# Two rounded 32-bit weight pieces and one set of 32-bit codes for the built units of pass 3

## What is computed

```
def _rgcn_conv(x, src, dst, edge_type, edge_weight, W, root, bias):
    xj = x[src]
    m = 0
    for r in range(4):
        mask = (edge_type == r)[:, None]
        m = m + mask * (xj @ W[r])
    m = m * edge_weight[:, None]
    out = segment_sum(m, dst, num_segments=6250)
    return out + x @ root + bias
...
ew = (edge_weight - edge_weight.min()) / (edge_weight.max() - edge_weight.min() + 1e-08)
h = relu(_rgcn_conv(x, src, dst, edge_type, ew, W1, root1, b1))
h = _rgcn_conv(h, src, dst, edge_type, ew, W2, root2, b2)
```

## Time and profile before

| | before |
|---|---|
| median of 3 runs (lowest, highest) | 3859.27 us (3858.65, 3859.64) |
| the profiled execution, its time | 3852.48 us |
| its span, first to last instruction | 3850.6 us |
| PE busy (matmul) | 3549.2 us, 92% |
| DVE busy | 2277.3 us, 59% |
| ACT busy | 2070.9 us, 54% |
| POOL busy | 2644.1 us, 69% |
| pass 0, first to last gather | 47.1 to 1116.4 us |
| pass 3, first to last gather | 1991.0 to 2928.5 us |
| pass 4, first to last gather | 2948.2 to 3836.4 us |

### The profile page before, as it was taken

How to read it: one execution, slowest core, us unless ns; L and a number is a source line. 1 busy time by engine, 2 the same in 40 slices (tenths; PEclk the granted TensorE clock), 3 DMA queues, 4 the chain that set the end, 5 groups by cost and what they waited for, 6 DMA issues and landing times. The chain is left out here.

```text
span 3850.6 us, 70135 instructions
## 1 busy us (share of the span) xinstructions
PE 3549.2 (92%) x23444; PEld 3114.6 (81%) x23444; DVE 2277.3 (59%) x7846; ACT 2070.9 (54%) x4844; POOL 2644.1 (69%) x2744
## 2 busy tenths in 40 slices
PE   7999999999999999799978998898986999989997
PEld 5999888888887999688856777777775888888887
DVE  6999998998876555666654445554442233333332
ACT  4555555555546555566665555555545445544543
POOL 5777777777753666355547777777776777777776
PEclk8999999999999999799989999999997889999898
DMA  7666666666675666466634454445443445555453
GB/s 232 190 190 191 185 191 190 185 188 191 184 206 133 162 161 161 116 161 167 160 103 158 162 169 168 168 166 170 168 163 125 154 155 170 161 159 170 150 170 119
DMA packets 438782, 642.44 MB, mean 167 GB/s; under 512 B 266434, under 2 KB 310978, under 8 KB 438275
## 3 DMA queue, kind: packets, MB, share of 16 engines
q1 hardware_dynamic: 310322, 375.66, 30.5%
q0 software_dynamic: 100880, 235.32, 22.7%
q10 hardware_dynamic: 27202, 26.78, 2.2%
HBM read 468.80 MB, written 168.73 MB: 166 GB/s over the span
## 5 line engine op out<-in xcount | busy, mean ns | idle before, releaser
L641 POOL DMA_INDIRECT work<-table_rel,reli x1462 | 1382.6, 946 | 493.9 <-issue 438.0
L641 POOL DMA_INDIRECT work<-table_pre,srci x831 | 817.3, 984 | 263.2 <-issue 261.0
L2582 ACT ACTIVATE work<-iota,local 128x72 f32<-128x72 f32 x1464 | 377.9, 342 | 322.8 <-PE bank L1589 313.7
L1589 PEld LDWEIGHTS bank<-work 128*128 128x128 f32 x2928 | 385.8, 210 | 190.9 <-DMA work<-table_rel,reli 185.4
L1589 PE MATMUL bank<-work 128*128 128x72 f32 x2928 | 398.7, 295 | 148.6 <-DMA work<-table_rel,reli 148.2
L2587 ACT ACTIVATE work<-work,ew,src_both 128x72 f32<-128x72 f32 x1464 | 514.9, 434 | 6.1
L1357 PE MATMUL bank<-counts,piece_hi 128*128 128x432 f32 x1300 | 482.9, 371 | 35.5 <-DVE counts L1307 23.5
L1019 ACT ACTIVATE X<-bank 128x468 uint8<-128x468 f32 (+1 forms) x624 | 326.6, 543 | 266.6 <-PE bank L961 259.8
L1357 PE MATMUL bank<-counts,piece_lo 128*128 128x432 f32 x1300 | 468.9, 361 | 0.0
L922 PE MATMUL bank<-w_both,work 128*128 128x256 f32 x1664 | 433.7, 386 | 17.5 <-DVE work L856 9.2
L934 PE MATMUL bank<-work 128*128 128x64 f32 x3328 | 399.6, 274 | 7.0 <-DVE hist L803 6.2
(11 more groups left out here) (322 smaller groups left out, 6129.6 us busy)
## 6 DMA issues: line engine op xcount, KB each, us to landing
work<-ea_cols SPq DMA_DIRECT2D x208, 256.0 KB, 2.9
kept<-work SPq DMA_DIRECT2D x50, 880.0 KB
kept<-w_both SPq DMA_DIRECT2D x50, 880.0 KB
work<-kept SPq DMA_DIRECT2D x50, 880.0 KB
w_both<-kept SPq DMA_DIRECT2D x50, 880.0 KB
adj<-X SPq DMA_DIRECT2D x156, 225.0 KB
work<-adj SPq DMA_DIRECT2D x65, 540.0 KB
work<-table_rel,reli POOLq DMA_INDIRECT x1462
```

The lines of the kernel that those rows point to most:

```text
L641: pool.indirect_dma_start(into[:, u, :], None, tables[p], bass.IndirectOffsetOnAxis(ap=idx_of(p)[:, t:t + 1].bitcast(U32), axis=0)).then_i ...
L1589: mm = pe.matmul(bank[4 + m % LATE_BANKS][:, 0:PAIR_WIN], late_gat[n % LATE][:, u, :], late_hot[:, n % LATE_HOTS, u * PAIR_WIN:(u + 1) * P ...
L2582: ins = act.activation(hot3[:, u, :], iota[:, 0:PAIR_WIN], ACT.Abs, bias=local[:, t:t + 1], scale=-1.0)
```

## The change

In pass 3 alone, the weight of an edge becomes two pieces instead of three: the value rounded to the 32-bit type that PE takes in one pass (`F32R`, fp32r in the profile), and the remainder, rounded to it again. So a tile has two low one-hots and two matmuls, and both operands are fp32r. Codes are written as fp32r too (`unit_code`, 1760 bytes a partition instead of 880), with one set of four buffers in place of two sets of bf16. Since there is one set, the codes of unit n are written when all four fills of unit n-1 are done, and `late_dve` calls `unit_take` of unit n-1 ahead of `unit_codes` of unit n instead of behind it. Buffers and `late_iota` move to other places; pass 4 keeps its bf16 pieces.

```
-        late_code = [x[:, at:at + CODE].bitcast(BF16)
-                     for x, at, n in ((work, 3072, 3), (work, 9600, 2), (work, 3732, 1), (work, 4864, 1), (src_hi, 0, 1))
-                     for at in range(at, at + n * CODE, CODE)]
+        unit_code = [nc.alloc_sbuf_tensor_at(f"unit_code{i}", [P, 2 * CODE], F32R, offset=at) for i, at in enumerate(
+            (work_at + 3072 * 4, work_at + 3512 * 4, work_at + 9600 * 4, src_both_at + TILES * 4))]
...
-        late_iota = src_hi[:, CODE:2 * CODE].bitcast(FP16)
+        lo_first = nc.alloc_sbuf_tensor_at("lo_first", [P, 12, P], F32R, offset=late_lo_at)
+        lo_last = nc.alloc_sbuf_tensor_at("lo_last", [P, 4, P], F32R, offset=work_at + 5088 * 4)
+        unit_lo = [[lo_first[:, i, :] for i in range(8)],
+                   [lo_first[:, i, :] for i in range(8, 12)] + [lo_last[:, i, :] for i in range(4)]]
+        unit_hi = nc.alloc_sbuf_tensor_at("unit_hi", [P, D_COLS], F32R, offset=b1a_row_at)
+        late_iota = work[:, 12544:12544 + CODE].bitcast(FP16)
...
+                if h - 1 in UNIT_AT:
+                    unit_take(p, UNIT_AT[h - 1], lambda to, x: dve.tensor_copy(to, x), dve)
                 if p == 3 and UNIT_AT.get(h, D_UNITS) < D_UNITS:
                     unit_codes(dve, UNIT_AT[h])
-                if h - 1 in UNIT_AT:
-                    unit_take(p, UNIT_AT[h - 1], lambda to, x: dve.tensor_copy(to, x), dve)
...
+            if len(w) == 2:
+                done(dve, dve.tensor_copy(unit_hi[:, :], rest_w))
+                done(dve, dve.tensor_tensor(w[1], rest_w, w[0], ALU.subtract))
+                return
...
-                for i in range(PIECES):
-                    dve.tensor_scalar(late_lo[:, half % 2, u * PIECES + i, :], iota_b[:, :], d_lo[:, at:at + 1],
+                for i in range(2):
+                    dve.tensor_scalar(unit_lo[half % 2][u * 2 + i], iota_b[:, :], d_lo[:, at:at + 1],
                                       d_w[i][:, at:at + 1], ALU.is_equal, ALU.mult)
...
-            if n >= 2:
-                dve.wait_ge(a_filled, FILLS_BEFORE + (n - 1) * U)
+            if n:
+                dve.wait_ge(a_filled, FILLS_BEFORE + n * U)
...
-                ins = dve.tensor_scalar(late_code[n % 2 * U + u], late_iota, float(hr * RHI * CW), d_code[:, first + u:first + u + 1],
+                ins = dve.tensor_scalar(unit_code[u][:, :], late_iota, float(hr * RHI * CW), d_code[:, first + u:first + u + 1],
                                         ALU.add, ALU.is_equal)
...
-                for i in range(PIECES):
-                    mm = pe.matmul(bank[A_BANKS_AT[u % 2]][:, 0:RHI * CW], late_lo[:, n // RANGES % 2, u * PIECES + i, :],
-                                   late_code[n % 2 * U + u], start=(i == 0), stop=(i == PIECES - 1))
+                for i in range(2):
+                    mm = pe.matmul(bank[A_BANKS_AT[u % 2]][:, 0:RHI * CW], unit_lo[n // RANGES % 2][u * 2 + i],
+                                   unit_code[u][:, :], start=(i == 0), stop=(i == 1))
```

More of the change, by code:

```diff
@@ L153, in gnn @@
         local = sb("local", [P, TILES])
+        src_both_at = -(-nc.sbuf_base // 32) * 32
         src_both = sb("src_both", [P, 2 * TILES])
@@ L183, in gnn @@
         B1B, B2A0, B2A1, GB, GBR, GAMMA, BETA, MB, RB1, RB2, U0 = range(11)
+        b1a_row_at = -(-nc.sbuf_base // 32) * 32
         b1a_row = sb("b1a_row", [P, HID])
@@ L241, in gnn @@
         CODE = RHI * CW // 2
-        late_code = [x[:, at:at + CODE].bitcast(BF16)
-                     for x, at, n in ((work, 3072, 3), (work, 9600, 2), (work, 3732, 1), (work, 4864, 1), (src_hi, 0, 1))
-                     for at in range(at, at + n * CODE, CODE)]
+        unit_code = [nc.alloc_sbuf_tensor_at(f"unit_code{i}", [P, 2 * CODE], F32R, offset=at) for i, at in enumerate(
+            (work_at + 3072 * 4, work_at + 3512 * 4, work_at + 9600 * 4, src_both_at + TILES * 4))]
+        late_lo_at = -(-nc.sbuf_base // 32) * 32
         late_lo = sb("late_lo", [P, 2, U * PIECES, P], BF16)
-        late_iota = src_hi[:, CODE:2 * CODE].bitcast(FP16)
+        lo_first = nc.alloc_sbuf_tensor_at("lo_first", [P, 12, P], F32R, offset=late_lo_at)
[4 more added lines that the diff above has]
+        late_iota = work[:, 12544:12544 + CODE].bitcast(FP16)
         d_code = src_hi[:, 2 * CODE:2 * CODE + D_COLS]
         d_lo = b2b_row[:, 0:D_COLS]
-        d_w = [b1a_row[:, i * D_COLS:(i + 1) * D_COLS] for i in range(PIECES)]
+        d_w = [unit_hi[:, :].bitcast(F32), b1a_row[:, D_COLS:2 * D_COLS]]
         d_sum = more[:, 0:2 * U * CW].rearrange("p (o c) -> p o c", o=2)
@@ L256, in gnn @@
         x_a = work[:, 4352:4352 + U * RHI * CW].rearrange("p (u t c) -> p u t c", u=U, t=RHI)
-        x_code = late_code[0:U]
+        x_code = [work[:, at:at + CODE].bitcast(BF16) for at in (3072, 3292, 3512, 9600)]
+        x_tmp = [view(9440 + i * X_COLS, X_COLS) for i in range(3)]
         x_sum = w_both[:, U * RHI * CW:U * RHI * CW + 2 * U * CW].rearrange("p (o c) -> p o c", o=2)
@@ L1413, in late_dve @@
                 if p == 3 and h == PAIRS // 2:
-                    built_setup(dve, in_extra, [x[:, 0:X_COLS] for x in d_tmp], x_first, x_lo, x_codes, x_w)
+                    built_setup(dve, in_extra, x_tmp, x_first, x_lo, x_codes, x_w)
                 if h >= LATE_LAG:
```

## The result

The changed kernel takes 3871.43 us (median of 7 runs, 3866.01 to 3876.26) against 3859.27 us (7 runs, 3856.52 to 3862.58): 1.0036 of the time before, 95% interval 1.0026 to 1.0046. It is slower by 12 us, where 19 were forecast. Its profiled execution took 3870.32 us with a span of 3868.5, against 3852.48 and 3850.6.

What follows compares the result with a forecast made beforehand. POOL's gather beat was taken to bound pass 3, with PE's savings and later codes worth 0. 100 units x 0.20 = 20 us, less about 1, gave +19 on 3859.3: 3878 us, range 3859 to 3890.

Steps and rivals of the forecast that it cites:

- POOL's beat bounds pass 3: Pass 3: one gather every 1.25 us sets the length; POOL never stops for a buffer, and PE waits for gathers.
- PE's saving is worth nothing: Fills of pass 3: fewer matmuls save PE 0.66 us a unit, hidden by POOL's beat; worth 0.
- 66 us: PE in pass 3: matmul time saved over 100 units, from half a fill taking 0.95 us instead of 1.28.
- 60 us or so: Sign to look for: PE's busy time falls by this much, and its waits for gathers rise by as much.
- The later codes are hidden: DVE in pass 3: codes queued behind the copies are ready 1.6 us before PE's next fill; worth 0.
- An fp32r code lasts 0.42 to 0.46 us: DVE in pass 3: length of one 440-column code, from a fixed 214 ns plus 0.46 to 0.56 ns a column.
- The price of a set of codes: Pass 3: four long codes lengthen POOL's gathers by 0.20 us a unit, priced from pass 0; +19 us in all.
- The rival that the codes stay harmless: Pass 3: pass 0's traffic lengthens gathers, or fp32r output slows DVE into a harmless mode; +0 to +3 us, chance 0.21.
- The upper bound: Pass 3: each code costs as much as pass 1's fp32r casts, 0.08 us, so 0.32 us a unit and 32 us.
- The rule: DVE and POOL share ports, held for a whole instruction; taken for the direction of the cost, not its size.

Runs made afterwards that it cites:

- e1: Kernel after, with the weight again in three bf16 pieces and matmuls, so only pass 3's codes are wider than before; 3874.2 us, 1.0031 of before.
- e2: Kernel after, with each 440-column code of pass 3 written by two DVE instructions of 220 columns; 3862.7 us, 1.0003 of before.
- e3: Kernel after, with each code of pass 3 made by a two-source DVE instruction instead of the one-source form; 3894.7 us, 1.0087 of before.
- e5: Kernel before, with one set of bf16 codes instead of two and copies of unit n-1 ahead of codes of unit n; 3859.8 us, 0.9995 of before.
- e6: Kernel before, with each code of pass 0 written in two DVE instructions of half the width; 1.0073 of before.
- e4: Kernel after, with the four codes of each unit in pass 3 written twice; 4883.1 us, 0.9992 of before.
- e12: Kernel before, with pass 0's codes split in halves, the same kernel as e6 run once more; 1.0025 of before.

## Why the prediction was right, point by point

- **POOL's beat bounds pass 3: right.** No wait of POOL for PE over 0.3 us in pass 3 before, after, or in e1, e2, e3 and e5, and pass 3's length followed the mean of the gathers in each (945, 965, 962, 945, 999, 947 ns give 937.5, 952.0, 950.1, 937.5, 977.6, 939.2 us).
- **PE's saving is worth nothing: right**, shown by e1, which gives it back and is as slow as after. **But 66 us was too much, for two reasons.** Half a fill takes 1.08 us (median), not 0.95: from the first matmul to the second it is 0.32 us and only then 0.20, where the sum had 0.197 for each step. So half a fill saves 0.20 us and the pass 40. And the granted clock of the pass, a mean over TensorE's two levels, fell from 0.95 to 0.92. Pass 3 as a whole, before and after, and what PE's gathered matmuls waited for the rows there, before, after and in e1:

```profile
1991.00:2930.00 939.00, 837.61 (x5139) 666.26 (x5139) 452.88 (x1313) 516.68 (x1647) 709.86 (x751) 0.95 0.48 162
1995.30:2948.70 953.40, 815.40 (x4739) 728.58 (x4739) 474.15 (x1229) 516.80 (x1646) 724.33 (x751) 0.92 0.48 160
PE bank L1589 <- DMA work<-table_rel,reli: 66.5, 49, 5.5
PE bank L1601 <- DMA work<-table_rel,reli: 102.6, 61, 4.2
PE bank L1601 <- DMA work<-table_rel,reli: 68.0, 48, 5.4
```

  PE's busy time fell by 22 us in the pass and by 28 in the whole kernel, where "60 us or so" was to be seen, and its waits for gathers rose by 36 us, not by as much as 60. With PE 3% slower at 0.92 than at 0.95, some 25 us of 815 (an estimate) went into the clock, and nobody waited for them: e2 has the same 0.92 and is level with before.
- **The later codes are hidden: right**, shown by e5.
- **An fp32r code lasts 0.42 to 0.46 us: right**, 444 ns.
- **The price of a set of codes was mis-sized.** The step took pass 0's mean, 0.20 us for each unit; measured are 0.145, and 14.5 us in place of 19. That is 4.5 of the 6.6 us between the forecast of 3878 and the median of 3871.4; the rest is within the spread of the runs. The median set costs the same in both, 0.145 us in pass 0 of the kernel before and 0.151 in pass 3 of the kernel after. But pass 0's mean, 0.193 by the same count, holds six sets of 0.5 to 0.96 us, and its smallest is 0.049, while in pass 3 the longest is 0.26 and 13 of 100 sets cost nothing. In the profile this shows as the longest gather, 1194 ns in pass 3 after, and in pass 0 of the kernel before 1905 ns, here in the list and then on the timeline beside its codes:

```profile
L641 POOL DMA_INDIRECT work<-table_pre,srci x831: 942/946/1905, 47.1 to 1116.4; - x167
65.45 1.91 POOL L641 DMA_INDIRECT work<-table_pre,srci  x1 [0.30 <-issue]
65.78 1.46 DVE L810 TENSOR_SCALAR X<-X 128x600 bf16<-128x600 f16 x4
```

  As in e6, a gather is held until a whole series of DVE instructions is through. There was luck in it too: the same pass 0 costs 0.193 us a set in this one trace and 0.20 to 0.245 in those of after, e1, e2, e3 and e5 (medians 0.145 to 0.152). Taken from any of these, the price would have been further off.
- **The rival that the codes stay harmless: wrong**, in both of its mechanisms. e1 and e2 lengthen and restore the gathers of pass 3 through the codes alone, with the traffic unchanged; and the codes did not slow down to 0.6 us, while e3, whose codes did, shows that this is not harmless in a two-source form.
- **The upper bound** (0.32 us a unit from the casts) was not reached, though e3 passed it with longer instructions. Its divisor came out right by chance: the 130 casts of the earlier trace rows are those with one of three inputs, over passes 1 and 2 together; by the trace pass 1 has 132 of all 260.
- **The rule** of the Trainium skill ("SBUF — State Buffer", section "Who interferes with whom"), that VectorE's two-port forms and GpSimd exclude each other for a whole instruction, gives the direction of after and e1. It doesn't give e2: eight instructions of the same form, 0.33 us each, left the gathers at 945 ns. The measurement decides: with gathers, length matters.

## What to carry to other kernels

Ask first which engine's beat sets a pass. Where it is POOL issuing indirect DMAs, the busiest engine's savings are worth nothing, and a wider type can cost time through the DVE instructions that write it, if single ones grow too long: here 0.33 us cost almost nothing and 0.38 us did cost. Cutting them into shorter ones won it all back in pass 3, but measure it in each pass, since in pass 0 it did not shorten the gathers. When a price is taken from another stage, look at its median and its tail, and not the mean alone.

## What the runs showed that I had not expected

- A two-source DVE instruction with both inputs in SBUF, writing SBUF, lengthens the gathers more than the one-source form (610 ns, 0.385 us a unit; gathers' mean 999 ns).
- A gather can be held through eight short DVE instructions in a row, for 1.07 us beyond its 0.94 (e6). This happened to between one series in nine and one in three, from one run of the same kernel to the next.
- The same program took a quarter longer in e4 and e6 to e12, with POOL off the path and the chain running through PE, DVE and a part that the profile doesn't name. What made it longer stays open. There the change, even with its codes doubled, was level with before (0.9985 to 0.9998), and with pieces of 320 and 120 columns 0.3% faster (0.9950 to 0.9995). Which of two kernels is faster can hang on that.
